# A four-layer graph network on Trainium2: the edge GRU and its products in f16 halves, the support turned, the third head's row maxima moved into the attention, exponent bits written by ScalarE, and the last weight applied before the last sum

## The reference

```python
# layer 1: x is layer 0's result
h = relu(layernorm(x)); d = diag(adj); A = adj - diag(d)
def gru(x, h, Wih, Whh, bih, bhh):       # gates r and z by sigmoid
    n = tanh(x @ Wih_n.T + bih_n + r * (h @ Whh_n.T + bhh_n))
    return (1 - z) * n + z * h
def head(W, a):                           # A @ hW gives each node's e
    e = leaky_relu(concat(A @ (h @ W), 0) @ a)
    att = softmax(where(A > 0, e[None, :], -9e15), axis=1)
    return att * A @ (h @ W)
edge = gru(A @ h, h, edge weights)        # A @ h is the "support"
node = gru((head0 + head1 + head2) / 3, h, node weights)
x = x + d[:, None] * (edge + node)
# layer 2
h = relu(layernorm(x))
x = x + concat(h, (adj @ h) / (adj.sum(1) + 1)) @ W.T
```

## Time and profile before

| | |
|---|---|
| median of 3 executions | 1450.34 us (1450.21 to 1451.42) |
| the profiled execution | 1448.13 us |
| its span, first to last instruction | 1446.3 us |
| mean granted TensorE clock | 0.943 |
| busy: PE, DVE, ACT, POOL | 1280.9, 1087.3, 722.1, 467.5 us |
| DMA | 146.71 MB, mean 101 GB/s |

### The profile page before, as it was taken

How to read it: one execution, slowest core, us unless ns; L and a number is a source line. 1 busy time by engine, 2 the same in 40 slices (tenths; PEclk the granted TensorE clock), 3 DMA queues, 4 the chain that set the end, 5 groups by cost and what they waited for, 6 DMA issues and landing times.

```text
span 1446.3 us, 35454 instructions
## 1 busy us (share of the span) xinstructions
PE 1280.9 (89%) x15174; PEld 1038.7 (72%) x15174; DVE 1087.3 (75%) x2025; ACT 722.1 (50%) x1106; POOL 467.5 (32%) x430
## 2 busy tenths in 40 slices
PE   2808899999998799999995999999999987879996
PEld 2708889999896576767663888888888543458885
DVE  4387998999842998899886778788796878854440
ACT  1459999999631123434424776556554224441110
POOL 4140000000110888788853500000700799810000
PEclk9958999999858999999997999999999999989998
DMA  9025554201216443444344201201100132036432
GB/s 306 29 95 151 183 163 132 65 19 41 69 82 165 150 136 124 137 136 142 124 164 172 64 2 55 68 1 49 55 2 20 61 106 95 15 130 191 162 121 79
DMA packets 71058, 146.71 MB, mean 101 GB/s; under 512 B 4461, under 2 KB 49379, under 8 KB 70127
## 3 DMA queue, kind: packets, MB, share of 16 engines
q1 hardware_dynamic: 69711, 143.86, 30.9%
q10 hardware_dynamic: 1184, 0.53, 0.1%
HBM read 129.88 MB, written 14.49 MB: 100 GB/s over the span
## 4 chain that ended last, share of the span: by engine, by line
PE 64%; DVE 12%; POOL 8%; ACT 6%; issue 5%; DMA 4%; SPq 1%; DVEq 0%; ACTq 0%; POOLq 0%
PE PS L1347 14%; PE PS L1480 9%; PE PS L1481 9%; PE PS L1381 6%; PE PS L1458 4%; PE PS L1543 4%; PE PS L1544 4%; PE PS L1430 3%; PE PS L1575 2%; PE PS L1422 2%; ACT arena L671 2%; PE PS L1423 2%; DMA arena<-in_adjT 2%; DVE arena L1154 2%; POOL arena L549 2%
## 5 line engine op out<-in xcount | busy, mean ns | idle before, releaser
L1480 PE MATMUL PS<-arena 128*128 128x257 f16 x1452 | 325.0, 273 | 14.2 <-ACT arena L765 11.4
L1481 PE MATMUL PS<-arena 128*128 128x257 f16 x1452 | 324.9, 274 | 0.0
L1347 PE MATMUL PS<-arena 128*128 128x65 f16 x7744 | 255.9, 195 | 58.6 <-DVE arena L960 46.0
L1347 PEld LDWEIGHTS PS<-arena 128*128 128x128 fp8e4 x7744 | 253.7, 99 | 60.8 <-issue 53.8
L1077 DVE CUSTOM_DVE_ANT_0 scratch<-arena 128x1408 bf16<-128x1408 f32 x132 | 231.6, 1754 | 39.1 <-POOL arena L560 22.6
L765 ACT ACTIVATE arena<-arena 128x896 bf16<-128x896 bf16 (+1 forms) x198 | 193.1, 983 | 122.9 <-PE PS L1481 91.4
L1154 DVE SCALAR_TENSOR_TENSOR arena<-arena,E,AT 128x896 bf16<-128x896 f32 (+1 forms) x198 | 229.6, 1213 | 28.4 <-ACT arena L765 20.9
L671 ACT ACTIVATE arena<-arena 128x1024 fp8e4<-128x1024 f32 (+1 forms) x185 | 187.2, 1089 | 4.9 <-DVE arena L954 4.4
L1480 PEld LDWEIGHTS PS<-arena 128*128 128x128 bf16 x1452 | 142.5, 98 | 38.6 <-issue 15.0
L1481 PEld LDWEIGHTS PS<-arena 128*128 128x128 bf16 x1452 | 139.8, 96 | 21.5
L954 DVE TENSOR_TENSOR arena<-arena,AT 128x256 int32<-128x256 int32 (+1 forms) x264 | 104.1, 394 | 23.4 <-ACT arena L671 21.3
(11 more groups left out here) (197 smaller groups left out, 2076.5 us busy)
## 6 DMA issues: line engine op xcount, KB each, us to landing
arena<-in_adj SPq DMA_DIRECT2D x88, 704.0 KB, 4.1
arena<-in_adjT SPq DMA_DIRECT2D x44, 512.0 KB, 4.5
hw_saved<-arena SPq DMA_DIRECT2D x22, 387.0 KB, 3.3
arena<-in_adjT SPq DMA_DIRECT2D x22, 384.0 KB, 4.3
arena<-hw_saved SPq DMA_DIRECT2D x2, 2838.0 KB, 11.2
arena<-e_rows SPq DMA_DIRECT2D x3, 1408.0 KB, 11.6
arena<-el_rows SPq DMA_DIRECT2D x8, 512.0 KB, 5.3
h_saved<-arena SPq DMA_DIRECT2D x1, 2816.0 KB, 8.1
```

What stands on the lines that cost most here:

```text
L1347: ins = pe.matmul(PS[:, k, q * C0:(q + 1) * C0], MASK[:, (m + j) % NMASK, q, k * P:(k + 1) * P], MOV[:, j, 2 * h + q, a, :], start=(j == 0 ...
L1480: pe.matmul(PS[:, k, 0:D + 1], weights, w[:, 0:D + 1], start=(j == 0), stop=False)
L1481: ins = pe.matmul(PS[:, k, 0:D + 1], weights, w[:, D + 2:2 * D + 3], start=False, stop=(j == NT - 1))
```

## The change

**Weights.** gat_W, the edge and node GRU's weights and W2 are cut by GpSimd into f16 halves in 12 pieces ahead of the edge loop, stored to DRAM and loaded again (`split`). h is turned once, as halves, and kept (HTS, HTN).

**Edge stage.** The support is made with h's half as the weights and AT as the moving matrix, 512 columns at a time for groups of four blocks (`support`, SUP), which gives it already turned. The products become a loop of their own ahead of the GRU, in halves, and the result is stored through a ring of two (HWS). The GRU (`gru_mm`) runs from the halves. VectorE takes the row maxima of heads 0 and 1 only, 2.5 adj half-rows per iteration. The blend moves from GpSimd to VectorE (`gru_blend`); GpSimd keeps three operations per block (`delta`, `apply`).

**Attention.** Head 2's row maxima are 44 passes on VectorE between the score operations, at m = 4, 6, ..., 90. ScalarE writes the exponent bits as int16 with one Relu at scale 16384 in place of the exponential; the mask turned in AT before (`turn_mask`, 66 operations of ScalarE) and turned back after (22 of VectorE) are gone.

**Node loop.** VectorE does gru_new of the same iteration's block, and the blend of the block before. The count is made in the first 20 rounds, each from one buffer, CK0. y = h2 @ W2 is made here for each normalised block, in halves (`turn`, `linear`, `product_high`, `product_low`), the half for the neighbours into YHL, the other added to X. NORM2 has five parts instead of three. The last stage only sums the neighbours' y: 44 matmuls of 256 columns for a block, and one operation of VectorE that scales and adds.

```diff
-    NORM2 = [(0, 11), (11, 17), (17, NT)]
+    NORM2 = [(0, 6), (6, 11), (11, 16), (16, 19), (19, NT)]
+    SUP = [(0, 4), (4, 8), (8, 12), (12, 16), (16, 20), (20, NT)]
+    HWPART = [(0, 6), (6, 12), (12, 18), (18, NT)]
...
+    def split(raw, half, scale, width):
+        link(pool.tensor_scalar(raw[:, 0:width], raw[:, 0:width], scale, 1.0, ALU.mult, ALU.mult))
+        link(pool.tensor_copy(half[:, 0, 0:width], raw[:, 0:width]))
+        pool.tensor_tensor(half[:, 1, 0:width], raw[:, 0:width], half[:, 0, 0:width], ALU.subtract
+                           ).then_inc(sem("ws"), 1)
...
-        pool.wait_ge(sem("n"), count)
-        link(pool.tensor_tensor(d, h_blk, n, ALU.subtract))
-        link(pool.tensor_scalar(trz[:, D:2 * D], trz[:, D:2 * D], 0.5, 0.5, ALU.mult, ALU.add))
-        link(pool.tensor_tensor(d, trz[:, D:2 * D], d, ALU.mult))
-        link(pool.tensor_tensor(d, d, n, ALU.add))
-        link(pool.tensor_scalar(d, d, DN[:, t:t + 1], 1.0, ALU.mult, ALU.mult))
-        pool.tensor_tensor(X[:, t, :], X[:, t, :], d, ALU.add).then_inc(sem("gru_x"), 1)
+    def delta(t, base, hr, n):
+        pool.wait_ge(sem(f"hr{t % 4}"), 16 * (saved_count(t % 4) + (t // 4 + 1) + (-(-(NT - t % 4) // 4) if base else 0)))
+        pool.wait_ge(sem("n"), base + t + 1)
+        pool.tensor_tensor(hr[:, t % 4, :], hr[:, t % 4, :], n[:, t % 2, :], ALU.subtract).then_inc(sem("delta"), 1)
+    def apply(t, base, hr):
+        pool.wait_ge(sem("blend"), base + t + 1)
+        link(pool.tensor_scalar(hr[:, t % 4, :], hr[:, t % 4, :], DN[:, t:t + 1], 1.0, ALU.mult, ALU.mult))
+        pool.tensor_tensor(X[:, t, :], X[:, t, :], hr[:, t % 4, :], ALU.add).then_inc(sem("gru_x"), 1)
...
-    def turn_mask(g, j):
-        blk = AT[:, j, G0[g][0] * P:(G0[g][0] + G0[g][1]) * P]
-        act.activation(blk, blk, ACT.Copy, scale=-MASKED, bias=MASKED, saturate=False).then_inc(sem("ab"), 1)
-                act.activation(PW[:, m % NRING, 0:nb * P], T[:, m % NRING, 0:nb * P], ACT.Exp, scale=LN2
-                               ).then_inc(sem("p_exp"), 1)
+        act.activation(PWb[:, m % NRING, 0:nb * P], T[:, m % NRING, 0:nb * P], ACT.Relu, scale=16384.0
+                       ).then_inc(sem("p_ready"), 1)
...
+        dve.tensor_copy(HWS[:, t % 2, :, :].rearrange("p h (a c) -> p h a c", a=2)[:, :, :, D], FRHL[:, t, :, :]
+                        ).then_inc(sem("hw_lo"), 1)
...
+    def row_max2(i):
+        t, c = divmod(i, 2)
+        dve.wait_ge(sem(f"arow{i % 3}"), 16 * (i // 3 + 1 + len(range(i % 3, 2 * NT, 3))))
+        if t // (NT // 2) == c:
+            dve.wait_ge(sem("row_diag"), NT + t + 1)
+        dve.wait_ge(sem("eb2"), 16)
+        dve.wait_ge(sem("rmax"), 4 * NT + i)
+        dve.tensor_tensor_reduce(junk, AROW2[:, i % 3, :], EB2[:, c * QUARTER:(c + 1) * QUARTER], 1.0, 0.0,
+                                 ALU.mult, ALU.max, M2[:, t, c, 2:3]).then_inc(sem("rmax"), 1)
...
+    def gru_new(t, base, trz, gt):
+        dve.wait_ge(sem("trz"), base + t + 1)
+        dve.wait_ge(sem("nb_mm"), base + t + 1)
+        if t >= 2:
+            dve.wait_ge(sem("blend"), base + t - 1)
+        nb_bank = PS[:, gates_bank(t, base) + 2, :]
+        link(dve.scalar_tensor_tensor(out=gt[:, t % 2, :], in0=trz[:, t % 2, 0:D], scalar=1.0, in1=nb_bank[:, D:2 * D],
+                                      op0=ALU.add, op1=ALU.mult))
+        dve.scalar_tensor_tensor(out=gt[:, t % 2, :], in0=gt[:, t % 2, :], scalar=0.5, in1=nb_bank[:, 0:D],
+                                 op0=ALU.mult, op1=ALU.add).then_inc(sem("u"), 1)
+    def gru_blend(t, base, hr, trz, gt):
+        dve.wait_ge(sem("delta"), base + t + 1)
+        d = hr[:, t % 4, :]
+        link(dve.scalar_tensor_tensor(out=d, in0=trz[:, t % 2, D:2 * D], scalar=1.0, in1=d, op0=ALU.add, op1=ALU.mult))
+        dve.scalar_tensor_tensor(out=d, in0=d, scalar=0.5, in1=gt[:, t % 2, :], op0=ALU.mult, op1=ALU.add
+                                 ).then_inc(sem("blend"), 1)
...
         dve.scalar_tensor_tensor(out=T[:, m % NRING, 0:nb * P], in0=MB[:, n % 2, 0:nb * P],
                                  scalar=E1B[:, j * H1 + h:j * H1 + h + 1], in1=AT[:, j, b0 * P:(b0 + nb) * P],
                                  op0=ALU.add, op1=ALU.min).then_inc(sem("t_built"), 1)
+        if m in row2_at:
+            row_max2(row2_at[m])
...
+    def product_low(b):
+        i = l2_order.index(b)
+        dve.wait_ge(sem("y_hi"), i + 1)
+        dve.scalar_tensor_tensor(out=YHL[:, b, 1, :], in0=PS[:, 6 + i % 2, 0:D], scalar=1.0 / W2SCALE,
+                                 in1=YHL[:, b, 0, :], op0=ALU.mult, op1=ALU.subtract).then_inc(sem("y_lo"), 1)
+        dve.scalar_tensor_tensor(out=X[:, b, :], in0=PS[:, 6 + i % 2, D:2 * D], scalar=1.0 / W2SCALE,
+                                 in1=X[:, b, :], op0=ALU.mult, op1=ALU.add).then_inc(sem("z_add"), 1)
...
-            link(dve.tensor_scalar(AT[:, t, :], AT[:, t, :], 0.0, None, ALU.is_equal, saturate=False))
-                                     op1=ALU.add, saturate=False).then_inc(sem("at_back"), 1)
-        if t >= 1:
...
+    for t in range(STEPS):
+        if t < NT:
+            dve.wait_ge(sem("sh_hi"), t + 1)
+            dve.tensor_tensor(ESH[:, t % 2, 2 * P:4 * P], PS[:, 0, 0:D], ESH[:, t % 2, 0:2 * P], ALU.subtract
+                              ).then_inc(sem("sh"), 1)
+            blk = AT[:, t, t * P:(t + 1) * P]
+            dve.scalar_tensor_tensor(out=blk, in0=ident[:], scalar=DN[:, t:t + 1], in1=blk, op0=ALU.mult,
+                                     op1=ALU.add, saturate=False).then_inc(sem("at_back"), 1)
+        if t < NT:
+            gru_new(t, NT, TRZ2, GT2)
+        if 1 <= t <= NT:
+            gru_blend(t - 1, NT, HR2, TRZ2, GT2)
+        for b in l2_at.get(t - 1, []):
+            product_low(b)
+        for b in l2_at.get(t, []):
+            low_half(b)
+        if NORM_LAG <= t < NT + NORM_LAG:
+            dve.wait_ge(sem("gru_x"), NT + t - NORM_LAG + 1)
+            norm_stats(2, t - NORM_LAG)
...
+    for t in range(NT):
+        dve.wait_ge(sem("agg"), t + 1)
+        if t == 0:
+            dve.wait_ge(sem("z_add"), NT)
+        dve.scalar_tensor_tensor(out=X[:, t, :], in0=PS[:, agg_bank(t), 0:D], scalar=RDEG[:, t:t + 1],
+                                 in1=X[:, t, :], op0=ALU.mult, op1=ALU.add).then_inc(sem("x_l2"), 1)
...
+    def support(s, c, j0, j1):
+        i0, i1 = SUP[s]
+        if s >= 2 and j0 == 0:
+            pe.wait_ge(sem("ns_lo"), DC * (s - 2) + c + 1)
+        for j in range(j0, j1):
+            for a in range(2):
+                ins = pe.matmul(PS[:, 2 * (s % 2) + c, 0:(i1 - i0) * P], HHL[:, j, a, c * P:(c + 1) * P],
+                                AT[:, j, i0 * P:i1 * P], start=(j == 0 and a == 0), stop=(j == NT - 1 and a == 1))
...
+    for t in range(NT):
+        if t >= 2:
+            pe.wait_ge(sem("hw_lo"), (H1 + 1) * (t - 1))
+        elif t == 1:
+            pe.wait_ge(sem("et"), 1)
+        bank = 6 if t % 2 == 0 else 4
+        for c in range(DC):
+            for a, b in TERMS:
+                st = HTS[:, t, (DC * a + c) * P:(DC * a + c + 1) * P]
+                pe.matmul(PS[:, bank, :], st, GWS[:, c, b, 0:2 * D], start=(c == 0 and a + b == 0),
+                          stop=(c == DC - 1 and a == 1))
+                ins = pe.matmul(PS[:, bank + 1, 0:D], st, GWS[:, c, b, 2 * D:3 * D], start=(c == 0 and a + b == 0),
+                                stop=(c == DC - 1 and a == 1))
+        ins.then_inc(sem("hw_mm"), 1)
...
+    def gru_mm(t, base, x_half, h_half, wih, whh, bias):
+        if t >= 2:
+            pe.wait_ge(sem("trz"), base + t - 1)
+            pe.wait_ge(sem("u"), base + t - 1)
+        bank = gates_bank(t, base)
+        for half, w, first in ((h_half, whh, True), (x_half, wih, False)):
+            for c in range(DC):
+                for a, b in TERMS:
+                    pe.matmul(PS[:, bank, :], half(c, a), w[:, c, b, 0:2 * D], start=(first and c == 0 and a + b == 0),
+                              stop=False)
+        pe.matmul(PS[:, bank, :], ones3[0:3, :], bias[0:3, 0:2 * D], start=False, stop=True).then_inc(sem("rz_mm"), 1)
+        for q, half, w in ((1, h_half, whh), (0, x_half, wih)):
+            o = PS[:, bank + 2, q * D:(q + 1) * D]
+            for c in range(DC):
+                for a, b in TERMS:
+                    pe.matmul(o, half(c, a), w[:, c, b, 2 * D:3 * D], start=(c == 0 and a + b == 0), stop=False)
+            ins = pe.matmul(o, ones3[0:3, :], bias[0:3, (2 + q) * D:(3 + q) * D], start=False, stop=True)
+        ins.then_inc(sem("nb_mm"), 1)
...
+    for s, (i0, i1) in enumerate(SUP):
+        if s + 1 < len(SUP):
+            for c in range(DC):
+                support(s + 1, c, 0, NT)
+        pe.wait_ge(sem("ns_lo"), DC * (s + 1))
+        for t in range(i0, i1):
+            gru_mm(t, 0, x_half, h_half, WIHS, WHHS, BIAS)
...
+    for t in range(STEPS):
+        blocks = l2_at.get(t - 1, [])
+        if blocks:
+            turn(blocks[0])
```

(15 more changed lines are left out.)

1305 lines of the change are left out of this document (685 added, 620 removed).

## The result

The changed kernel takes 1636.57 us (median of 4, 1634.56 to 1637.83), the kernel before 1450.88 (1450.21 to 1451.54): a ratio of 1.129, 95% interval 1.1265 to 1.1316. It is slower, as forecast, but by 186 us and not by 116; it lies above the range of 1510 to 1600. Its profiled execution took 1635.6 us with a span of 1633.5, and a mean granted clock of 0.889.

The account below looks back on a forecast made before the run. TensorE was taken to bound the edge and attention loops, with three engines close in the node loop. 1448.1 + 4 - 22.6 + 40.5 + 94.6 = 1564.6, plus half of 2.2, gave 1566 us; range 1510 to 1600.

Parts of the forecast that it names:

- The node loop's alternation: Node loop: TensorE and VectorE take turns, 9.7 us a round against 6.97, or 11.15 with a slow restart.
- The rival in which it doesn't bind: Node loop: TensorE runs at its own pace, 7.05 us a round, whole kernel 1440; chance 0.08.
- The rival of a slow write: Attention: ScalarE's int16 write takes up to 2.0 us, adding 45; with a colder clock, over 1600, chance 0.08.
- The 35 us for the products with W2 in the node loop: Node loop: last-weight products cost 27 us of operations and low halves, plus 8 for TensorE's turns and waits.
- the four terms: Before the edge loop +4, edge stage -22.6, attention +40.5, node loop and last stage +94.6 us.
- (d) From there VectorE is full: Edge stage, after second support and one GRU step: VectorE bounds the rest, 192 us in all.
- From m=91 TensorE leads: 107 steps, 175, and 2 at the end: Attention, steps behind the third head's passes: TensorE sets the pace, 175 us, plus 2 at the end.
- from m=5 ... 181: Attention, steps with the third head's passes: 181 us with TensorE waiting for VectorE, 186 with GpSimd's diagonals.
- Before the edge loop: +4 (0 to +8): Ahead of the edge loop: GpSimd's weight splits cost 4 us, by late transfers among the casts of h.
- Six pieces lie in its pause of 30.5 us: Ahead of the edge loop: six weight pieces fit GpSimd's pause and cost nothing; 21 us without that cover.
- So a round with a gap of 4.3 restarts slow: +1.45, 11.15.: Node loop: TensorE's 4.3 us idle lowers its clock, adding 1.45 to a 9.7 us round, making 11.15.
- a colder clock: Rival, node loop: each step wholly at half speed, +3.5 a round, 1600 to 1640; with slow ACT, chance 0.08.

Follow-up runs that it names:

- e11_products_late: Changed kernel with all repairs and row maxima moved forward, node loop taking one normalised block a round, its product a round later: 1447.2 us, ratio 0.9973.
- e3: Changed kernel with the edge loop's adj half-rows asked for ahead of the reload of h: 1611.1 us, ratio 1.1122.
- e2: Changed kernel with the next unit's spread row maxima asked for at step 12 instead of step 21: 1620.1 us, ratio 1.1187.
- e6: Changed kernel with GpSimd's three splitting operations per weight piece replaced by one memset, results wrong: 1624.0 us, ratio 1.1185.
- e7: Changed kernel with 18 unread 512-column matmuls added behind each of the first ten node-loop GRU steps: 1623.8 us, ratio 1.1211.
- e4: Kernel before, with its node loop doing gru_new and ScalarE's gates of block t right behind sh(t): 1538.8 us, ratio 1.0628.
- e12: Changed kernel, all repairs, one late product a round, no row maxima between edge products, 4 half-rows more ahead of first gru_new: 1449.5 us, ratio 0.9983.

## Why the prediction was right and wrong

**Right: the direction, and its mechanism.** The node loop's alternation was the largest term. It shows in the timeline, it goes when gru_new is moved back, and it comes when the kernel before gets the same order. The rival in which it doesn't bind is out: the node round is 11.6 us, far from 7.5. The length of a round at full clock (9.7 forecast, 9.5 with the gap filled), the pass of 1.60, the products' 2.9 us a block (66.8 us for 22, so 3.0, and ScalarE waits 26.1 of them for a store), the last stage at 4.9 a block (its last 812 matmuls take 88.8 us), and the int16 write (0.985 us) came as said. The rival of a slow write is out with it. The 35 us for the products with W2 in the node loop came as said too: rounds 9 to 20 take 33 more than twelve rounds of 11.6. But they aren't needed: one block a round, taken up later, took 32 away (`e11_products_late`).

**Wrong: the size, outside the range.** The forecast of 1566 was 71 us short. It is no single step; the four terms fell short by 13.6, 18.8, 26.0 and 12.3 us. Two of them, the edge stage and the attention, left out the same thing, the place of a transfer in SP's queue. The other two were mis-sized. Term by term:

- *"(d) From there VectorE is full".* It was not: it waited for adj rows that SP asked for behind the reload of h, which waits for a block's end. This had no price in the sum. It measured 20.7 us (e3), and the edge stage without it is 325 to 327, the forecast's 327. That agreement isn't luck: in e3 the support alone takes 21.3 (forecast 22.5), from there to the first gru_new 90.0 (89), and the rest 213.7 (215.6).
- *"From m=91 TensorE leads: 107 steps, 175, and 2 at the end", and "from m=5 ... 181".* The spread maxima had no price either. They are asked for at a unit's last step, behind requests that wait for passes or for TensorE; 19.6 us (e2). Without them the attention is 46.9 us longer than before, against the 40.5 forecast. The steps with passes are then even shorter than forecast (190 us against 194) and those behind them longer (190 against 177); of this no run shows the cause.
- *"Before the edge loop: +4 (0 to +8)".* It was 17.6, of which e6 gives 12.5 to the splits. The price of a split came out right (3.5 forecast, 3.6 measured), though the earlier trace rows alone would give 6.0 for nine times 256 elements, so that hit is in part luck. But six of them among the casts of h don't only cost where a transfer is late: each cast behind a split is late, some 6 us in the end. "Six pieces lie in its pause of 30.5 us" was wrong as well; they stand among the casts of AT before that pause (18.6 to 47.4 us), and layer 0 starts later for them.
- *"So a round with a gap of 4.3 restarts slow: +1.45, 11.15."* The right mechanism, 2.1 in place of 1.45 (e7). After the longer gap the twelve matmuls took 3.9 to 5.3 us and not 4.2, as in the earlier trace rows. As the round at the upper clock was 9.5 and not 9.7, it came to 11.6, 0.4 over the forecast; over 22 rounds this is some 9 of the 12.3 us by which the stage is over. No run places the rest. The Trainium skill, "TensorE: Matmul & The Clock Gate", section "HAM oscillation — how this bites in real kernels", which was weighed there, states that every such burst starts at the low clock; the runs agree for the gap of 4.2 us (3.9 us and more in each round with it, 2.75 with it filled), but not for one of 2.10 (2.76 and 4.45 in e4).

The range's upper end took in a colder clock only as one case of 0.08, and gave nothing to waits that come of the new order of SP's requests. The prediction read the new order of VectorE and TensorE and not SP's.

**What the change would give with its losses repaired.** In e12's profile the stretches differ from the kernel before by +19 (to the support), -29 (edge), +39 (attention, to sh(0)) and -27 (from sh(0) to the end, 299.8 against 326.8): +2 in all. So the edge stage and the last two gain 56 us; the attention, in which TensorE was full and which now holds the 44 passes, and the stretch with the splits lose 58. How the gain divides between the f16 halves, the early last weight and the work that fell away no run shows.

## What to carry to other kernels

Before an operation that waits is put behind another in a loop, write down for both engines who waits for whom in one round: if the result that starts the next round stands behind the operation that ends this one, the engines take turns, and here the idle half also cost the clock. Then read the DMA-issuing engine's queue in the same way, since a request behind a wait is as late as that wait, and a removed stall uncovers it. Price work on a helper engine at what stands behind it in its own queue, not at its own length against that engine's idle total.

## What the runs showed of the hardware

- Filling TensorE's idle time with matmuls that nothing reads made the kernel 13 us faster: twelve matmuls went from 3.9 to 5.3 us (a part at the lower of the two clocks; granted 0.81 over these rounds) to 2.75, all at the upper one (granted 1.00).
- With gaps of 2.10 us ahead of them, twelve equal matmuls took 2.76 us in one round and 4.45 in the next (e4_before_serial, 1146.93 and 1154.64): the gap just ahead of a burst doesn't decide alone. A gap of 4.3 gave 3.93 and 5.28 in two neighbouring rounds.
- GpSimd's multiplication L700 takes 0.46 us in some places and 1.84 to 1.87 in others, where VectorE is in a row maximum or the count; VectorE's row maxima take 1.62 to 2.04. The changed kernel's group (lowest/median/highest ns), and one case:

```profile
L700 POOL TENSOR_SCALAR arena<-arena,DN x44: 464/1842/1869, 580.2 to 1491.2; 128x256 f32<-128x256 f32 x44
```

```profile
1310.80 1.61 DVE L1381 SCALAR_TENSOR_TENSOR scratch<-arena 128x1408 fp8e4<-128x1408 f32 x1
1310.89 1.86 POOL L700 TENSOR_SCALAR arena<-arena,DN 128x256 f32<-128x256 f32 x1
```

The Trainium skill, "SBUF — State Buffer", section "Who interferes with whom", says that a VectorE instruction with two inputs in SBUF contends with a GpSimd instruction that reads SBUF. That fits: the row maximum and the count have two such inputs, and in this case GpSimd's operation starts 0.09 us behind VectorE's and ends 0.34 us behind its end. No run here separates the port from other causes.
